# Cross-attention megakernel on one core: Gram results in rising order, diagonal blocks in tiles of their own, masked out of PSUM

## The reference: what is computed

```python
q, k_t, v_t = heads(x @ W_q), heads(text @ W_k), heads(text @ W_v)
probs_t = softmax(q @ k_t.T * 0.25)                 # 20 heads, 112 x 371
text_out = probs_t @ v_t
qsem = l2norm(probs_t @ text)                       # 512 wide for every head and query
sem = qsem @ l2norm(ip).T                           # 4 columns
probs_ip = softmax(q @ k_ip.T * 0.25 + 0.5 * sem) * spatial_mask
out = (text_out + probs_ip @ v_ip) @ W_out + b_out + x
```

## Time and profile before

| | |
|---|---|
| median of 3 runs | 390.13 us (387.19 to 395.4) |
| the profiled execution | 389.0 us, of which the span of instructions is 387.0 us |
| mean granted TensorE clock in it | 0.974 |
| TensorE busy | 358.2 us, 93% of the span, 3498 matmuls |
| VectorE busy | 269.1 us, 70% |
| ScalarE busy | 215.7 us, 56% |
| GpSimd busy | 213.1 us, 55% |

### The profile page before, as it was taken

How to read it: one execution, slowest core, us unless ns; L and a number is a source line. 1 busy time by engine, 2 the same in 40 slices (tenths; PEclk the granted TensorE clock), 3 DMA queues, 4 the chain that set the end, 5 groups by cost and what they waited for, 6 DMA issues and landing times.

```text
span 387.0 us, 9366 instructions
## 1 busy us (share of the span) xinstructions
PE 358.2 (93%) x3498; PEld 304.9 (79%) x3498; DVE 269.1 (70%) x566; ACT 215.7 (56%) x490; POOL 213.1 (55%) x230
## 2 busy tenths in 40 slices
PE   8999799995899979999899979998999899999886
PEld 7879599874788868888788878886888678877664
DVE  4897673693667695587858685687758587867464
ACT  6734133783557455647556554757455458557741
POOL 8020271397138861596438662696349615865872
PEclk9999999998799989999999989999999999999899
DMA  8999993259105802265205702283203710002001
GB/s 265 313 240 188 249 188 105 64 169 157 23 1 158 155 13 59 81 142 103 75 5 176 134 22 65 82 179 63 77 3 103 128 42 3 2 3 58 0 3 31
DMA packets 30145, 38.01 MB, mean 98 GB/s; under 512 B 14394, under 2 KB 27307, under 8 KB 29419
## 3 DMA queue, kind: packets, MB, share of 16 engines
q1 hardware_dynamic: 29732, 37.00, 41.1%
q10 hardware_dynamic: 368, 0.41, 0.3%
HBM read 28.49 MB, written 8.81 MB: 96 GB/s over the span
## 4 chain that ended last, share of the span: by engine, by line
PE 64%; DVE 16%; DMA 9%; issue 6%; SPq 3%; ACT 1%; POOL 0%; DVEq 0%; ACTq 0%
PE PR L1127 32%; PE Y L1127 18%; PE O L1127 7%; PE P L1127 5%; DVE mx L1001 4%; DMA qst<-ma 3%; DVE dl L974 3%; DMA tri<-tri_d 2%; DMA big<-xT 2%; DVE pb L1025 2%; DVE ssq L885 1%; DMA kd<-ks 1%; PE PR L1326 1%; DVE cTl L1101 1%; SPq L519 1%
## 5 line engine op out<-in xcount | busy, mean ns | idle before, releaser
L633 POOL TENSOR_TENSOR pb<-pb 128x448 f32<-128x448 f32 x78 | 91.2, 1170 | 99.9 <-DVE pb L1025 96.9
L1001 DVE TENSOR_REDUCE mx<-PR 112x1 f32<-112x371 f32 x160 | 81.6, 536 | 50.5 <-PE PR L1127 49.5
L1025 DVE TENSOR_TENSOR pb<-big,Y 128x448 f32<-128x448 f32 x120 | 73.5, 617 | 32.1 <-PE Y L1127 30.5
L813 ACT ACTIVATE big<-P 128x448 f32<-128x448 f32 x120 | 64.7, 539 | 55.0 <-PE P L1127 55.0
L1127 PE MATMUL Y<-er,Gh 128*128 128x448 f32 x240 | 93.4, 413 | 1.7 <-ACT er L817 1.4
L817 ACT ACTIVATE er<-big 128x448 fp32r<-128x448 f32 x120 | 69.4, 578 | 3.8
L1127 PE MATMUL P<-qst,kst 99*128 99x112 bf16 x480 | 44.0, 218 | 9.4 <-DMA qst<-ma 9.0
L1127 PEld LDWEIGHTS Y<-er,Gh 128*128 128x128 f32 x240 | 46.1, 192 | 8.0 <-issue 2.3
L1127 PE MATMUL PR<-kst,qst 96*112 96x371 bf16 x160 | 48.7, 329 | 2.5 <-DVE mx L1001 2.1
L1127 PEld LDWEIGHTS P<-qst,kst 99*128 99x128 bf16 x480 | 30.6, 101 | 25.1 <-issue 17.8
L1127 PE MATMUL Y<-er,Gl 128*128 128x448 f32 x120 | 44.4, 370 | 0.0
(11 more groups left out here) (208 smaller groups left out, 719.1 us busy)
## 6 DMA issues: line engine op xcount, KB each, us to landing
et<-ctxT SPq DMA_DIRECT2D x7, 752.0 KB, 4.9
kst<-kd SPq DMA_DIRECT2D x7, 720.0 KB, 7.4
kd<-ks SPq DMA_DIRECT2D x16, 288.0 KB, 2.9
qst<-qd SPq DMA_DIRECT2D x48, 70.0 KB, 3.5
kst<-kd SPq DMA_DIRECT2D x7, 480.0 KB, 9.5
kst<-kd SPq DMA_DIRECT2D x9, 240.0 KB, 9.1
qd<-kst SPq DMA_DIRECT2D x4, 336.0 KB, 7.8
vx<-xr SPq DMA_DIRECT2D x8, 140.0 KB, 2.5
```

The costliest lines, as they stand in the source:

```text
L633: pool.tensor_tensor(total, total, (pz, pm)[j], ALU.add).then_inc(s_S, 1)
L813: act.activation(e, P[(3 * g + c) % 2][:, 0:448], ACT.Exp).then_inc(s_exp, 1)
L1001: dve.tensor_reduce(mx[b % 2][:, h:h + 1], bank[0:S, 0:T], AX.X, ALU.max).then_inc(s_free[seq[u] % NR], 1)
L1025: dve.tensor_tensor((pz, pm, pa[g % 2])[j], eb[g % 3][:, 448 * j:448 * j + 448], Y[y % 2][:, 0:448], ALU.mult).then_inc(s_P, 1)
```

## The change

Five things are changed together.

1. The Gram results of a group are made in the order 0, 1, 2 (1, 3 and 5 matmuls) instead of 2, 1, 0. Result j waits for chunk j of `er` alone, where before the first (j = 2) waited for all three chunks.
2. The diagonal blocks have tiles of their own, `W[0]` and `W[1]` (128 x 3 x 128). The last matmul of each Gram result reads `W` instead of the first columns of `Gh`.
3. For batches 1 to 7 the mask is multiplied out of the PSUM bank by `upper`, in `G` and `GV`, just ahead of the subtraction that makes `Gl`: three VectorE operations for each batch (128, 128 and 115 columns). Line 980 is left for batch 0 only, and writes `W[0]`.
4. The order tables are written anew: `D` of batch 0 goes behind the third maximum, `Kr` goes from the start of the fourth round to the third (for batch 2 to the end of the second one), `wo` (the split of the output weights) two thirds of a round earlier, `E` is split in `Ea` and `Eb` and goes behind g1, `L` and the last `St` go ahead of `o`, and g2 of the last group goes behind `o`.
5. Two more fills on GpSimd at the start set `W` to zero.

```diff
-FILLS = 28
+FILLS = 30
-ROUNDS = ("K0 S0 m g2 m g1 S1 m K1 m S2 m g0 v G0",
-          "S0 m g2 g1 m S1 m g0 K2 C v m S2 G1 m",
-          "S0 m g2 T0 T1 g1 m g0 r0 S1 m pw S2 m v V0 m",
-          "Kr r1 m g2 g1 S0 m m g0 V1 S1 m m S2 v r2 mT z GV",
-          "p g2 pT E g1 D cT S0 S1 v g0 L o S2")
+ROUNDS = ("K0 m S0 m g0 g1 S1 m K1 S2 m g2 m v G0",
+          "g0 S0 m m g1 g2 S1 m m K2 C v S2 G1 m",
+          "Kr S0 m g0 m T0 T1 g1 g2 S1 r0 pw m S2 m v V0",
+          "m g0 g1 S0 m r1 m m g2 V1 S1 m S2 m v r2 mT z GV",
+          "p g0 pT g1 Ea Eb D cT S0 S1 v L S2 o g2")
-LATE = "p g2 pT g1 S0 g0 D cT S1 L S2 v o"
-LAST = ("S0 S1 v g2 S2 g1 T0 T1 g0",
-        "S0 r0 g2 g1 pw v S1 g0 pv S2",
-        "S0 r1 g2 S1 r2 g1 g0 S2 v",
-        "S0 g2 S1 z g1 p g0 S2 v",
+LATE = "p g0 pT D g1 g2 cT L S0 S1 v S2 o"
+LAST = ("S0 v g0 S1 g1 T0 g2 S2 T1",
+        "g0 r0 S0 g1 v pw S1 g2 pv S2",
+        "r1 S0 S1 g0 g1 r2 g2 S2 v",
+        "S0 g0 S1 g1 z p S2 g2 v vW",
...
-    order += [("D", 0)]
-    side = [("V", 0, 1), ("L", 0), ("V", 0, 2)] + [("qip", b) for b in range(B)]
+    side = [("V", 0, 1), ("D", 0), ("V", 0, 2), ("L", 0)] + [("qip", b) for b in range(B)]
...
+            def upper(b, i, bank, o):
+                if i == 0 and b >= 2:
+                    dve.wait_ge(s_gram, 3 * NG * (b - 1))
+                n = min(128, T - 128 * i)
+                dve.tensor_tensor(W[b % 2][0:n, i, 0:n], bank[0:n, o:o + n], tri[0:n, 0, 0:n], ALU.mult)
...
-                    diag = Gh[b % 2][:, :, 0:128]
-                    dve.tensor_tensor(diag, diag.bitcast(f32), tri[:, 0, :].unsqueeze(1).broadcast_to([128, 3, 128]),
-                                      ALU.mult).then_inc(s_wu, 1)
+                    if b == 0:
+                        dve.tensor_tensor(W[0][:, :, :], Gh[0][:, :, 0:128].bitcast(f32),
+                                          tri[:, 0, :].unsqueeze(1).broadcast_to([128, 3, 128]), ALU.mult)
...
-                    if j == 2:
-                        pe.wait_ge(s_er, 3 * g + 3)
+                    pe.wait_ge(s_er, 3 * g + j + 1)
...
-                    mm(d, Gh[b % 2][:, j, 0:128], er[g % 2][:, 448 * j:448 * j + 448], j == 0, True).then_inc(s_gram, 1)
+                    mm(d, W[b % 2][:, j, :], er[g % 2][:, 448 * j:448 * j + 448], j == 0, True).then_inc(s_gram, 1)
```

More of the change, by code:

```diff
@@ L125, in master_schedule @@
                 if w == "g":
-                    order += [("gram", g, j) for j in (2, 1, 0)]
+                    order += [("gram", g, j) for j in range(3)]
                 elif w in ("g2", "g1", "g0"):
@@ L130, in master_schedule @@
                     order += [u for u in [next(maxes, None)] if u and n < B]
-                elif w == "E":
-                    order += split(b + 3) if b + 3 < B else []
+                elif w in ("Ea", "Eb"):
+                    order += split(b + 3)[2 * (w == "Eb"):][:2] if b + 3 < B else []
                 elif w in unit:
@@ L218, in build @@
         Gl = [sb(f"Gl{i}", [128, 3, TP], f32r) for i in range(2)]
+        W = [sb(f"W{i}", [128, 3, 128], f32r) for i in range(2)]
         dl = sb("dl", [128, 3, 128], f32r)
@@ L571, in _ @@
                 fill(Gl[i][:, :, :].bitcast(f32), 0.0)
+                fill(W[i][:, :, :].bitcast(f32), 0.0)
             fill(tn_[:, C:384], 0.0)
@@ L626, in _ @@
                             pool.wait_ge(s_km, b)
-                if u[0] == "gram" and u[2] < 2 and u[1] < NG * B - 1:
+                if u[0] == "gram" and u[2] and u[1] < NG * B - 1:
                     g, j = u[1], u[2]
                     total = pa[g % 2]
-                    pool.wait_ge(s_P, 3 * g + 3 - j)
-                    if j == 0:
+                    pool.wait_ge(s_P, 3 * g + j + 1)
+                    if j == 2:
                         pool.wait_ge(s_S, 2 * g + 1)
-                    pool.tensor_tensor(total, total, (pz, pm)[j], ALU.add).then_inc(s_S, 1)
+                    pool.tensor_tensor(total, total, (pm, pz)[j - 1], ALU.add).then_inc(s_S, 1)
                 if u[0] == "C":
@@ L954, in _ @@
                     gh, gl = [p[b % 2][0:r, i, 0:T - 128 * i] for p in (Gh, Gl)]
+                    if b:
+                        upper(b, i, bank, 0)
                     dve.tensor_tensor(gl, bank[0:r, 0:T - 128 * i], gh.bitcast(f32),
@@ L963, in _ @@
                     gh, gl = [p[b % 2][0:r, 2, 0:a] for p in (Gh, Gl)]
+                    upper(b, 2, bank, C)
                     dve.tensor_tensor(gl, bank[0:r, C:C + a], gh.bitcast(f32), ALU.subtract).then_inc(s_free[seq[u] % NR], 1)
@@ L1016, in _ @@
                     g, j = u[1], u[2]
[L1017 removed]
+                    y = 3 * g + j
                     dve.wait_ge(s_gram, y + 1)
@@ L1020, in _ @@
                         dve.wait_ge(s_pa, len(posp))
-                    if j == 2 and g >= 2:
+                    if j == 0 and g >= 2:
                         dve.wait_ge(s_pv, g - 1)
-                    if j < 2 and g:
-                        dve.wait_ge(s_S, 2 * g - j)
-                    dve.tensor_tensor((pz, pm, pa[g % 2])[j], eb[g % 3][:, 448 * j:448 * j + 448], Y[y % 2][:, 0:448],
+                    if j and g:
+                        dve.wait_ge(s_S, 2 * g - 2 + j)
+                    dve.tensor_tensor((pa[g % 2], pm, pz)[j], eb[g % 3][:, 448 * j:448 * j + 448], Y[y % 2][:, 0:448],
                                       ALU.mult).then_inc(s_P, 1)
@@ L1281, in _ @@
                     b, r = divmod(g, NG)
-                    y = 3 * g + 2 - j
+                    y = 3 * g + j
                     if y >= 2:
                         pe.wait_ge(s_P, y - 1)
-                    if j == 2 and r == 0:
+                    if j == 0 and r == 0:
                         pe.wait_ge(s_wd, b + 1)
-                    if j == 2:
-                        pe.wait_ge(s_er, 3 * g + 3)
+                    pe.wait_ge(s_er, 3 * g + j + 1)
                     d = Y[y % 2][:, 0:448]
```

10 lines of the change are left out of this document (5 added, 5 removed), and 10 rows, old and new, of tables (EARLY, LAST).

## The result

The changed kernel takes **369.7 us** (median; 369.2 to 369.9), the one before 389.7 on the same chip: a ratio of **0.951, 95% interval 0.946 to 0.955**. Forecast were 377 and a range from 370 to 388; the median lies 0.3 under its lower end. The ratio is of fast executions, and so without the 395.4 us of the kernel before, which ran in the slower state. The two profiled executions take 389.0 and 369.9, 19.1 less, where the sum of the prediction had 13.0.

The account below looks back on a forecast made before the run. TensorE bounds the kernel (busy 358.2 of 387.0 us), so only its idle time and low-clock stretches can give time. Terms 2.6 + 1.7 + 6.4 + 3.4 + 1.5 - 2.6 = 13.0 us off 390.1 give 377, range 370 to 388.

Parts of the forecast that it names:

- The signs that were named: Signs of a right forecast: no o wait over 0.3, pT wait about 0.5, last maximum about 55, first wait 3.7, clock 1.00.
- Prologue: Start, D of batch 0 behind three maxima: VectorE's idle time goes and one maximum comes earlier, gain 2.6 us.
- Keys of batch 2: First boundary, St waiting for ma: the kst load leaves earlier, gain 1.7 of the 5.35 us wait.
- the two reasons given: For the earlier kst load: wol no longer gates it (0.95 us), and K stands two maxima earlier (0.75 taken).
- four slow stretches: Work at 1.2 GHz after TensorE idled, at 40 to 50, 140, 220 and 355: 1.7 us lost at each.
- Boundaries and clock of the middle four batches: Six boundaries gain 6.4 us, mainly o's waits for cTl going; full clock after the waits at 140 and 220 gains 3.4.
- the small waits: New waits from re-ordering 35 rounds with maxima, banks coming late: 2.6 us lost, 0.07 a round, ends 0 and 7.
- `upper` at nothing: Three upper operations ahead of Gl, 0.8 us per batch on VectorE, costed at nothing because TensorE works elsewhere.
- The last batches and the tail: Last two boundaries: St's waits for ma go, 2.6 to 2.7 us; last batch: half of er wait plus slow clock, 1.5.
- Rival 4: VectorE still held: dl behind GpSimd's sum and first el, o waits as now; 3 gained, 387 us, chance 0.09.
- Rival 1: The load takes VectorE's place: the chain keys, kd, kst, ma sets the boundaries; 6 gained, 384 us, chance 0.23.
- Rival 2: All terms at their good ends, no new small waits, part of the prologue's clock: 18 gained, 372 us, chance 0.10.

Follow-up runs that it names:

- the mask behind `Gl`: Changed kernel with each masking operation behind its Gl, out of Gh in SBUF, not ahead of it out of the bank: 370.8 us, ratio 0.951.
- the mask at `D`: Changed kernel and its order, but the mask multiplied out of Gh in SBUF into W in one pass at D, all batches: 370.7 us, ratio 0.946.
- g1 moved ahead: Changed kernel with g1 of the third round moved ahead of one maximum and the two T: 372.4 us.

## Why the prediction was right, and where not

The direction and the main mechanism held: TensorE's idle time at the boundaries went, because what `cTl` stands behind on VectorE came out of GpSimd's way, and the clock came back with it: of the 19.4 us by which the span fell, 12.1 are idle time of TensorE and 7.3 its busy time. The signs that were named did show, two of them in another size: no wait of `o`, a wait at `pT` (0.17 at most, for 0.5), clock 1.00, the last maximum near 55 (55.7), a shorter first wait (1.83, for 3.7). Against the ledger, by its steps:

- **Prologue: 2.6 forecast, 1.5 measured** (57.34 to 55.85), and hardly by the step that was named; that something like it came out is luck. The waits of 1.40 and 1.38 took the place of the one for the mask; `D` moved back costs 0.2 there. What differs is the clock, for which the prediction counted nothing at this place. The kernels with the prologue of before had their first transposition at 56.1 with the clock at 1.00 throughout, at 57.3 with 3.4 us at 1.2 GHz, at 58.4 with 6.8 and at 60.5 with 10.2. With the new prologue it came at 54.8 to 55.9 at full clock in all traces but one, and at 56.8 in that one (the mask behind `Gl`), with 3.4 us at 1.2 GHz. Whether the new place of `D` is what keeps the clock up is not shown: the old place kept it up once. From the first to the second transposition the changed kernel takes 0.5 us more (30.8 to 31.3), which stands in no term.
- **Keys of batch 2: 1.7 forecast, the wait is shorter by 3.5** (5.35 to 1.83). The load left 3.0 earlier, 1.5 of it with the prologue and 1.5 for the two reasons given (0.8 for the gate, 0.7 for `K`); `ma` landed 4.4 earlier.
- **The missed term: the slow stretch behind the first boundary.** The spacing from the second to the third transposition fell by 5.0 (44.1 to 39.1), of which the wait is 3.5. Where the clock fell there in later kernels it took 41.0 (the mask at `D`), 1.8 more. The prediction had counted four slow stretches, and this fifth was the longest.
- **Boundaries and clock of the middle four batches: 8.7 measured.** Forecast was 6.4 for all six boundaries and 3.4 for the clock; without the 2.6 of the last two and with four sevenths of the small waits' 2.6 that is 5.7. Three sizes were off. `pT` waited 0.11 to 0.17 for 0.5: `pe_` runs beside the first matmul of g0 (both at 128.94) and not 0.3 behind it as in the earlier trace rows. The later waits for `ma` went instead of growing. And the small waits were 2.4 us there, four of 0.59, above the 1.5 allowed.
- **`upper` at nothing** was right, for a reason I had not given. Each wait of 0.59 holds one masking operation (0.28), which the prediction had said would lie "while TensorE works elsewhere"; that was wrong. But taking it out of the way gives nothing back, in two kernels. The Trainium skill ("VectorE: DVE Perf Modes", the TRN2 errata) gives each VectorE operation a fixed part, by which three small operations cost an estimated 0.3 more than one. The trace agrees in the difference, 0.28 + 0.28 + 0.28 for the 0.55 of line 990, though each is longer than the estimate from the page (0.26 and 0.46). VectorE is still busy 2.3 us less: `dl` takes 6.1 less over the run and the masking 3.1 less, while the multiply in `L`, now beside the `el` passes, takes 5.6 more.
- **The last batches and the tail: 4.1 forecast** (2.6 and 1.5), 4.6 measured (37.2 to 34.9, 46.5 to 44.2). The wait of 1.37 for `er` went, but one of 1.14 came, which was in no term. VectorE stands 2.07 for GpSimd at `zm` with a product queued behind it (timeline of the changed kernel):

```profile
344.63 1.97 POOL L665 TENSOR_TENSOR t<-ssq,halfm 112x10 f32<-112x10 f32 x1
...
347.47 0.23 DVE L1105 TENSOR_REDUCE zm<-z 112x20 f32<-112x80 f32 x1 [2.07 <-POOL z L697]
...
348.29 0.47 PE L1137 MATMUL Y<-er,Gh 128*128 128x448 f32 x1 [1.14 <-DVE pb L1035]
```

- **The rivals.** Rival 4 (VectorE still held) did not come about, since `dl` got in 0.16 ahead of GpSimd's sum; made on purpose the hold costs some 2 us at four boundaries (3.3 with a slow stretch elsewhere), and not the 10 between its 387 and the forecast. That kernel has no line 980 to be held as well, which I take for the reason, and its `dl` is held by the `el` pass alone. That VectorE is held for as long as GpSimd has work was the prediction's own reading of "contends": `dl` was let go after the pass under way each time. Rival 1 holds at the first boundary alone. Rival 2 (372) was the nearest in size, but by luck: it had no new small waits, and six of 0.59 came.

## What to carry to other kernels

Ask what a VectorE operation with both inputs in SBUF meets when it becomes ready: begun just ahead of a long GpSimd operation it costs its own time, begun just behind it costs what is left of that operation too. Then see what waits for it: a held operation that nothing waits for, as the multiply in `L` here, costs nothing. Either move it or take one such operation off the path; the second remedy adds nothing to the first. When a wait is long, look at the clock behind it as well, at every such place and not at the ones that the slices happen to show; and before a transfer is moved behind another, find its first reader.

## What the runs showed of the hardware

- `dl` (128x384, both inputs in SBUF) took 0.55 when it started 0.16 us ahead of a GpSimd sum, and the sum took 1.39 for 1.15 then; it took 2.03 when it started 0.16 behind the first `el` pass. A reduction with one SBUF input (`lh`) took 0.55 every time. The multiply in `L` (128x384, both inputs in SBUF) took 0.56 to 0.59 in all eight cases before and up to 1.79 after, beside the `el` passes. The masking operation out of PSUM took 277 to 293 ns in all 21 cases of the changed kernel, out of SBUF (the mask behind `Gl`) 267 to 611.
- The length of a wait alone does not tell whether the clock falls. At the first boundary waits of 1.83, 1.88, 2.10 and 2.12 left it at 1.00, waits of 1.81, 1.87, 2.06 and 2.08 were followed by 1.2 GHz. In the kernel before, 1.95 and 2.06 for `cTl` were followed by it and 2.15 for `ma`, at 309.93, was not. What TensorE did before them differs only in small ways, and I found no sign that tells them apart. A stretch behind the wait of 2.10 (g1 moved ahead), and one behind 1.87 (the mask at `D`):

```profile
94.00:102.00 8.00, 8.00 (x79) 7.24 (x81) 5.61 (x11) 5.98 (x13) 3.35 (x3) 1.00 0.20 50
```

```profile
94.00:102.00 8.00, 8.00 (x46) 7.45 (x46) 4.68 (x10) 4.33 (x10) 2.62 (x3) 0.79 0.12 32
```
